# Value and row-sum matmuls of an attention set side by side behind its four scores, in a two-layer transformer kernel

## The reference

```python
scores = jnp.einsum('bhqd,bhkd->bhqk', Qr, Kr) * DH ** (-0.5)
scores = jnp.where(causal, jnp.finfo(scores.dtype).min, scores)
pattern = jax.nn.softmax(scores, axis=-1)
heads = jnp.einsum('bhqk,bhkd->bqhd', pattern, Vh).reshape(b, t, d)
...
xn = _layernorm(x, axis=-1)
x = x + _L0_attn_ref(xn, ...) + _L0_ffn_ref(xn, ...)
xn = _layernorm(x, axis=-1)
x = x + _L1_attn_ref(xn, ...) + _L1_ffn_ref(xn, ...)
```

## Time and profile before

| | |
|---|---|
| time, median of 3 runs | 2285.57 us (2283.03 to 2285.79) |
| profiled execution, span | 2287.4 us |
| PE busy | 2116.6 us, 93% of the span |
| DVE, ACT, POOL busy | 51%, 32%, 30% |
| mean granted TensorE clock | 0.979 |

### The profile page before, as it was taken

The page is one execution under the profiler, slowest core; times in us unless marked ns, Lnnn a source line. Parts: engine busy times, 40 slices in busy tenths (PEclk is TensorE's granted clock), DMA queues, the critical chain, the costliest instruction groups (busy, mean ns, idle before and its releaser), DMA issues.

```text
span 2287.4 us, 35555 instructions
## 1 busy us (share of the span) xinstructions
PE 2116.6 (93%) x11200; PEld 1390.8 (61%) x11200; DVE 1159.1 (51%) x1946; ACT 739.0 (32%) x1357; POOL 680.0 (30%) x428
## 2 busy tenths in 40 slices
PE   4999999999889999999969999999998999999997
PEld 3756656566475656576557566665765756475764
DVE  5534636355445546464356255462645546382733
ACT  3242242423323333423322423324233232424232
POOL 3314323142221414142323142331422314041523
PEclk9999999999999999999979999999998999999998
DMA  3303103141021303040123031130411303030403
GB/s 134 79 29 93 42 22 82 32 111 43 19 73 44 79 28 96 10 115 29 51 101 95 11 93 43 41 85 11 120 34 37 79 20 97 10 96 10 124 21 127
DMA packets 72439, 141.10 MB, mean 62 GB/s; under 512 B 9328, under 2 KB 26736, under 8 KB 71152
## 3 DMA queue, kind: packets, MB, share of 16 engines
q1 hardware_dynamic: 72304, 139.25, 21.9%
HBM read 75.77 MB, written 4.19 MB: 35 GB/s over the span
## 4 chain that ended last, share of the span: by engine, by line
issue 73%; POOL 25%; POOLq 1%; DMA 0%; SPq 0%; ACT 0%
POOL hl L716 5%; POOL swapped L722 4%; POOL pr L728 3%; POOL wgl L693 3%; POOL wul L693 2%; POOL wdl L693 2%; POOL wqkl L693 2%; POOL al L732 2%; POOL raw L709 1%; POOL wol L693 1%; DMA tt<-in_wdown_dram 0%; POOL QS L701 0%; POOLq L715 0%; POOLq L711 0%; POOLq L725 0%
## 5 line engine op out<-in xcount | busy, mean ns | idle before, releaser
L629 ACT ACTIVATE pr<-S 128x512 f32<-128x512 f32 (+3 forms) x768 | 342.2, 489 | 316.5 <-PE S L958 217.2
L847 DVE TENSOR_TENSOR xres<-D,xres 128x512 f32<-128x512 f32 x352 | 242.3, 688 | 370.2 <-PE D L879 364.0
L716 POOL TENSOR_TENSOR hl<-tt,hh 128x512 fp32r<-128x512 f32 x108 | 138.8, 1285 | 872.8 <-ACT hh L653 872.5
L955 PE MATMUL S<-QS,KS 98*128 98x512 f32 (+2 forms) x768 | 267.4, 411 | 19.8 <-ACT pr L629 11.0
L955 PEld LDWEIGHTS S<-QS,KS 98*128 98x128 f32 x768 | 145.1, 192 | 188.3 <-ACT pr L629 165.5
L653 ACT CAST hh<-tt 128x512 fp32r<-128x512 f32 x108 | 67.0, 620 | 488.8 <-DVE tt L861 488.8
L821 DVE TENSOR_REDUCE mp<-S 128x1 f32<-128x128 f32 (+3 forms) x384 | 176.7, 484 | 71.7 <-PE S L937 61.2
L837 DVE RECIPROCAL denom<-denom 128x256 f32<-128x256 f32 x64 | 109.0, 1729 | 186.4 <-ACT denom L636 186.4
L879 PE MATMUL G<-xh,wgh 128*128 128x512 f32 x432 | 180.0, 417 | 19.1 <-issue 13.8
L879 PE MATMUL D<-wdh,hh 128*128 128x512 f32 x432 | 183.8, 426 | 4.1 <-DVE xres L847 3.0
L879 PE MATMUL G<-xh,wgl 128*128 128x512 f32 x432 | 178.2, 412 | 0.0
(11 more groups left out here) (145 smaller groups left out, 3794.1 us busy)
## 6 DMA issues: line engine op xcount, KB each, us to landing
KS<-pr SPq DMA_DIRECT2D x192, 128.0 KB, 2.3
QS<-pr SPq DMA_DIRECT2D x192, 128.0 KB, 2.3
raw<-in_wgate_dram SPq DMA_DIRECT2D x29, 512.0 KB, 4.2
raw<-in_wup_dram SPq DMA_DIRECT2D x28, 512.0 KB, 3.7
raw<-in_wdown_dram SPq DMA_DIRECT2D x28, 512.0 KB, 3.5
raw<-in_wqk_dram SPq DMA_DIRECT2D x18, 512.0 KB, 3.5
vh<-val SPq DMA_DIRECT2D x16, 512.0 KB, 3.9
val<-in_x_dram SPq DMA_DIRECT2D x6, 1024.0 KB, 11.0
```

What stands on the lines that cost most here:

```text
L629: act.activation(pr[:, (i * HG + h) % 8, skip:W], S[h % 2][:, skip:W], ACT.Exp, scale=SCALE) \
L716: pool.tensor_tensor(hl[:, fc, :], tt[:, (blk * nfc + fc) % 2, :], hh[:, fc, :].bitcast(F32), ALU.subtract) \
L847: dve.tensor_tensor(xres[:, rt, :], d[:, :], xres[:, rt, :], ALU.add).then_inc(sem["v_dfree"], 1)
L955: ins = pe.matmul(s[:, first:W], KS[0:SHIFT, h, kb * P:(kb + 1) * P], QS[0:SHIFT, h, c * W + first:(c + 1) * W], start=True, stop=not masked)
```

## The change

Both quads of a set move to the end of the second half, so that the list has four scores (with MLP work between the halves, where there is any) and then eight 32-wide matmuls in a row. The wait of the value quad changes with it: four exps back from its new place in place of two, which is the same exp.

```diff
@@ weighted
         scores = [("st", i, h) for h in range(HG)] if i < len(SETS) else []
-        now = [scores[:2] + [("pv", i - 1)], scores[2:] + [("sums", i - 1)]]
+        now = [scores[:2], scores[2:] + [("pv", i - 1), ("sums", i - 1)]]
@@ pv (tensor engine)
-                pe.wait_ge(sem["a_exp"], n("a_exp", -2 if i < len(SETS) - 1 else 0))
+                pe.wait_ge(sem["a_exp"], n("a_exp", -HG if i < len(SETS) - 1 else 0))
```

## The result

| | before | after |
|---|---|---|
| time, median of four runs each | 2285.68 us (2283.03 to 2286.77) | 2344.78 us (2341.96 to 2347.76) |
| ratio, 95% interval | 1 | 1.0263 (1.0248 to 1.0277) |
| profiled execution, span | 2287.4 us | 2344.4 us |
| mean granted clock | 0.979 | 0.975 |

A forecast was written before the change was run, and what follows sets the result against it. PE, busy 93% of the span, was taken to bound the kernel. Lost exp cover of 66.1 us less 11.8 gained gave +54.3 on the 2287.4 span, 2341.7; less 1.8 for timed runs, 2340, range 2318 to 2364.

The forecast's parts named there:

- The wait: Sign of being right: PE's wait for exps rises from 11 to some 60 to 80 us, busy time within some 15.
- Switches: One entry and exit between full and 32-wide matmuls vanish per set: 0.31 unmasked, 0.25 masked, 50 us gross gain.
- Filled sets: Sets with MLP work between the halves: the third score stays covered and the gain is kept; 11.8 us with last pairs.
- The side-by-side quad: A 512-wide quad directly followed by another: 0.88 us before the next quad starts, bounds 0.85 and 0.99.
- Unfilled, unmasked: Sets without mask or MLP piece between halves: third score waits for the first's exp; 4.12 against 3.31, +0.81 each.
- Masked sets: Unfilled sets with a mask, same uncovered exps: +0.56 (set 8), +0.45 (9), +0.39 (2 and 10), +0.29 (3 and 11).
- Set 4: PE waits there already before the change; only the 128-wide quad is put behind: +0.24 each, 3.9 us in 16 sets.
- Set 1: In twelve loop turns its exps stand behind an ACT cast, so a whole quad's cover goes without a gain: +0.88 each.
- Set 11 where it is unfilled: Masked set with 128-wide exps and 256-wide quads, no MLP piece between halves: +0.29, or +0.18 in tails.
- The clock: Rival, more slower: set 1 of each of twelve loop turns draws a 1.2 GHz stretch; +20 us, 2360; chance 0.13.
- Time given back: Rival, less slower: stops let DVE catch up, shrinking PE's residual-add waits; at most 25 us back, 2315; chance 0.04.
- The range: 2318 to 2364, from the quad pair's bounds (-5, +19), an entry error behind stops (-11), and low clock.

The follow-up runs named there:

- its padded form: The changed kernel with 256 already fulfilled semaphore waits put ahead of PE's loops; 2316.66 us, ratio 1.0138 to the kernel before.

## Why the prediction was right

- **The wait.** Named: 60 to 80 us in well over 100 cases; measured 73.7 in 136. Busy time was to stay within 15 us of before: it is 3.9 less.
- **Switches.** Filled sets 0.31 shorter: sets 6 and 7 of turn0 -0.36 and -0.33, masked set 9 -0.29 (0.25 forecast), set 5 there -0.16 (0.12). The gain is real and was costed well; it stands in too few sets.
- **The side-by-side quad.** 0.88 to 0.89 as taken. The pair's exit was a little cheaper than I had it, 0.97 to 0.98 for 0.99.
- **Unfilled, unmasked.** +0.81 forecast, +0.79 to +0.80 in turn1, +0.80 and +0.72 in tail0. The whole chain of set 4 carried over, the third score 1.33 behind the first (752.88 - 751.55) where 1.34 was read from set 4.
- **Masked sets.** +0.56, +0.45, +0.39, +0.29 forecast for sets 8, 9, 2 and 10, 3; measured +0.53, +0.44, +0.37, +0.27. All a hair high, by the 0.02 of the exit and some 0.01 more.
- **Set 4** +0.24, measured +0.25. **Set 1** +0.88 in loops, measured +0.85 to +0.90 where the clock stayed up. I had read its old stop (0.72) in turn1 alone; turn0's was 0.41, and the price came out the same, as the whole cover goes either way.
- **Mis-sized.** Set 11 where it is unfilled: +0.29 and +0.18 forecast, +0.05 and +0.06 measured, 1.7 us in eight sets. The term left out that the old order had a small stop at the very end: before, one 256-wide quad stood between the last score and the value quad that needs its exp, and held PE 0.65 (to 764.23), 0.06 behind the end of the last exp (763.59 + 0.58):

```profile
763.58 0.64 PE L979 MATMUL E<-pr,ones 128*32 128x256 f32 x8
...
763.59 0.58 ACT L629 ACTIVATE pr<-S 128x128 f32<-128x128 f32 x2 [0.61 <-PE S L958]
```

  After, two quads stand there, and the same quad holds PE 0.43:

```profile
776.63 0.61 PE L979 MATMUL E<-pr,ones 128*32 128x256 f32 x8
777.06 0.40 PE L972 MATMUL O<-pr,vh 128*32 128x128 f32 x8
```

  In tail1 set 10 came at +0.07 for +0.2, and set 11 with its last pair at -0.68 for -0.52 (0.25 and 0.27). The gain of the other filled sets was 1 us more than forecast. Together with the hundredths above, the sum was some 5 us high.
- **The clock.** The forecast left it out and the rival had twelve such stretches, 20 us, each behind some 1.8 us without a matmul; the stops were that long only in turn1. Five came, 7.5 us, less the one that went. Without both, the inside would be at 55.4 - 7.5 + 1.4 = 49.3, where I had 54.3; that the two errors cancel is luck. So is part of the rest: the jump-back stops, which the sum had not, added some 4 us to the measured 59, against a forecast of 54.
- **Time given back.** Refuted: PE's wait for the residual add is 18.2 where it was 18.4.
- **The range.** Its ends don't follow from the bounds beside it: -5 and -11 together give 2324, not 2318, and the clock rival 2360, not 2364. The measured 2344.8 lies inside either way.

The switch to 32 columns: the Trainium skill, "TensorEngine Tiling (Array Packing)", section Key Properties, has changing the mode drain the engine. By that rule, the trace agrees: a pair that is entered and left once in place of twice saves 0.3 us where nothing else stops PE. The section gives no size, so where the prediction says that the trace agrees in size, the 0.3 us is the trace's alone. On small stops and the clock: 132 stops of up to 0.8 us in the kernel with all but set 1 brought no lower clock among the scores; stops of 1.4 us did in one of six turns and stops of 1.8 us in four of six. The rule of the Trainium skill, "TensorE: Matmul & The Clock Gate", section A second HAM failure mode: psum-queue depth-cycling, does not show here for groups of matmuls as near together as these.

**What stays open.** Why set 1's stop is followed by the lower clock in five turns of twelve in the changed kernel and in three in its padded form, and what decides about the stops of the last section.

## What to carry to other kernels

Before moving an operation to save a switch, ask what it covers: with two banks, the third score needs the first one's exp, and for a 512-wide score a chain of 1.2 to 1.3 us (score, way there, exp, way back) must lie under something. The quad of 1 us that stood there was nearly free, for PE would have waited in its place; moving it lost 0.8 a set, and the same move wins 0.3 a set where other work stands in the gap, so decide it set by set and bring the work there first. Price such a change from the one place in the old trace where the cover is already too short: here set 4, which foretold the 18 sets 5 to 7 of turn1 within 0.02.

## What the runs showed of the hardware that I had not expected

At the jump back of turn0's loop PE may stop for 3.1 to 4.7 us and then run at the lower clock level for a few more, 5 to 6.6 us each, 21 in the kernel before and 25 in the changed one: a hundredth of it, and more than most edits are worth. It comes with instruction packets of 16 KB (1.49 MB / 91), nine for each jump back: 91 or 92 in all, against 55 or 56 without the stops. Within turn1's shorter loop no such packet comes and PE does not stop so. The Trainium skill, "Runtime: NRT & Kernel Launch", section Instruction fetch mechanics, says that a taken branch whose target lies outside the current two-page window forces a fetch before execution can go on, and gives 128 KiB for PE, in blocks of 16 KiB. The trace agrees in that the stop and the packets come together, but not on two pages: an iteration of turn1's loop has some 1300 rows of PE in the trace (matmuls, weight loads and the sequencer's), by the page's 256 instructions a block an estimate of five blocks or more, and it jumps back without one packet. What decides it is not settled. 256 more instructions ahead of the loops take the stops away, 64 don't; but the kernel of before with short exps lost all four with PE's program unchanged, and one kernel kept one of four, so the place of the loop in PE's own program is not the whole cause. Nor was it traced whether the stops come and go between two executions of one kernel; the ten times of the kernel with both quads behind two scores, 2275.3 to 2291.3 us, and one of the four with all but set 1, 12 us below the rest, leave that open.

For experiments it means this: two kernels that differ by some 5, 10 or 20 us outside the place of the edit should first be compared in their instruction packets. Two of my expectations failed by 28 and 22 us mainly for this, and a third in part, while the distances inside the stretches had moved as the theory says.
